# Axial attention in a ten-layer kernel: six SBUF-to-SBUF transfers for the maxima's rows, scores eleven steps behind, and the last scores in two pairs of PSUM banks

## The reference, cut to what matters

```python
q = (x @ Wq).reshape(b, n, 32, 8)
k, v = jnp.split(ctx @ Wkv, 2, axis=-1)      # each to (b, n, 32, 8)
q = apply_axial_rope(q, pos_map)
k = apply_axial_rope(k, ctx_pos_map)
logits = jnp.einsum('bqhd,bkhd->bhqk', q, k) * scale
w = jax.nn.softmax(logits, axis=-1)
attn = jnp.einsum('bhqk,bkhd->bqhd', w, v)
return attn.reshape(b, n, 256) @ Wout + bout
```

## Time and profile before

| | |
|---|---|
| median of 3 runs | 1564.13 us (1559.62 to 1566.8) |
| the profiled execution | 1560.38 us |
| its span, first to last instruction | 1558.6 us |
| PE, DVE, ACT busy over the whole span | 86%, 68%, 49% |
| mean granted TensorE clock | 0.928 of full speed |
| step -1 to the layer's last add | about 366 us to 533.9 us of the span |

### The profile page before, as it was taken

The page is one execution under the profiler, slowest core; times in us unless marked ns, Lnnn a source line. Parts: engine busy times, 40 slices in busy tenths (PEclk is TensorE's granted clock), DMA queues, the critical chain, the costliest instruction groups (busy, mean ns, idle before and its releaser), DMA issues.

```text
span 1558.6 us, 21496 instructions
## 1 busy us (share of the span) xinstructions
PE 1342.1 (86%) x6925; PEld 938.8 (60%) x6925; DVE 1053.0 (68%) x2217; ACT 761.3 (49%) x1887; POOL 209.0 (13%) x221
## 2 busy tenths in 40 slices
PE   8678759986898656899999779994999999869998
PEld 4344345553444334567676579983888888754554
DVE  6888968888776587788877533225666666666564
ACT  5677822445786474655554212223666666512221
POOL 0122220000000000312111064111111111010000
PEclk8799979996899887999999889997999999969999
DMA  5122140000000200000002179854211211000110
GB/s 194 68 95 81 75 189 1 0 1 1 5 4 5 78 0 1 1 1 34 35 1 79 38 281 332 300 206 159 102 67 67 74 67 61 34 0 17 33 33 27
DMA packets 36418, 111.02 MB, mean 71 GB/s; under 512 B 4693, under 2 KB 15966, under 8 KB 30992
## 3 DMA queue, kind: packets, MB, share of 16 engines
q1 hardware_dynamic: 34464, 105.75, 19.3%
q0 software_dynamic: 1872, 4.22, 0.7%
HBM read 84.66 MB, written 26.21 MB: 71 GB/s over the span
## 4 chain that ended last, share of the span: by engine, by line
PE 69%; DVE 16%; ACT 6%; issue 6%; DMA 2%; DVEq 0%; SPq 0%; POOL 0%; ACTq 0%; POOLq 0%
PE psum L3044 6%; PE psum L2356 5%; PE psum L2695 4%; PE psum L1938 4%; PE psum L871 4%; PE psum L2643 3%; PE psum L2673 3%; PE psum L1980 3%; PE psum L2721 3%; DVE roomA L752 3%; PE psum L3054 3%; PE psum L2365 2%; PE psum L1329 2%; PE psum L1970 2%; PE psum L2651 2%
## 5 line engine op out<-in xcount | busy, mean ns | idle before, releaser
L2760 ACT ACTIVATE roomA<-psum,roomA 128x256 f32<-128x256 f32 x128 | 71.0, 560 | 92.6 <-DVE roomA L2825 92.3
L1496 DVE TENSOR_REDUCE roomB<-psum 128x2 f32<-128x512 f32 x128 | 83.7, 688 | 35.9 <-PE psum L1329 34.8
L2026 ACT ACTIVATE roomA<-psum,roomA 128x128 f32<-128x128 f32 (+1 forms) x128 | 53.4, 427 | 88.3 <-DVE roomA L2101 88.1
L3044 PE MATMUL psum<-roomA,roomB 128*128 128x512 f32 (+1 forms) x192 | 89.4, 609 | 0.3 <-ACT roomA L3151 0.3
L2495 DVE SCALAR_TENSOR_TENSOR roomA<-roomA,psum 128x512 f32<-128x512 f32 x23 | 15.9, 690 | 99.1 <-ACT roomA L2400 99.1
L505 PE MATMUL psum<-roomB,own 128*128 128x256 f32 x256 | 64.9, 403 | 15.6 <-ACT roomB L604 15.3
L1938 PE MATMUL psum<-own,roomB 128*128 128x512 f32 x160 | 75.0, 594 | 3.4 <-DVE roomA L2093 2.1
L1901 POOL TENSOR_TENSOR roomA<-roomA 128x512 f32<-128x512 f32 x40 | 50.7, 1268 | 176.8 <-DVE roomA L2094 169.7
L505 PEld LDWEIGHTS psum<-roomB,own 128*128 128x128 f32 x256 | 50.8, 202 | 38.1 <-ACT roomB L604 20.6
L2695 PE MATMUL psum<-roomA 128*128 128x256 f32 x256 | 68.3, 389 | 6.0 <-DVE roomA L2837 4.4
L752 DVE TENSOR_TENSOR_SCAN roomA<-roomA 128x1024 f32<-128x1024 f32 x32 | 73.1, 2284 | 0.0
(11 more groups left out here) (509 smaller groups left out, 3396.5 us busy)
## 6 DMA issues: line engine op xcount, KB each, us to landing
roomB<-m_w_dram SPq DMA_DIRECT2D x12, 1536.0 KB
roomA<-m_w_dram SPq DMA_DIRECT2D x11, 1536.0 KB
a_kv_ready<-roomB SPq DMA_DIRECT2D x32, 512.0 KB, 3.1
roomA<-a_kv_ready SPq DMA_DIRECT2D x8, 1024.0 KB, 4.8
roomA<-a_kv_ready SPq DMA_DIRECT2D x16, 512.0 KB, 4.2
roomB<-a_w_dram SPq DMA_DIRECT2D x4, 1280.0 KB, 6.2
roomB<-f_w_dram SPq DMA_DIRECT2D x8, 624.0 KB, 3.8
m_rows<-roomA SPq DMA_DIRECT2D x1, 2978.5 KB, 15.7
```

Source lines behind the costliest of these rows:

```text
L1496: dve.tensor_reduce(maxneg[:, hp // 8, :, m, hp % 8], g.bank(m).rearrange("p (q k) -> p q k", k=S), AX.X, ALU.max, negate=True).then_inc(s ...
L3044: ins = pe.matmul(g.bank(bank, rows=m), w[:, kt, at:at + m], xg[:, n % 2, kt, half * HALF:(half + 1) * HALF], start=(kt == 0), stop=(kt == ...
```

## The change

- The DRAM tensor and the transfer into it go. Instead of store, wait and two loads, SP issues six transfers straight from `partsT` to `trQ`: one for each head m and part c, each from 8 partitions of 512 bytes into one partition's row of 4096 bytes. All six count on the same semaphore as the loads did (96 instead of 32 a batch).
- LAG goes from 13 to 11, so there are 83 steps instead of 85; scores, exponentials, `weigh`, `back` and `keep` all move two steps earlier against the maxima. M entries come one step earlier, in even steps (8, 16, ..., 64), behind the T entry of that step where there is one.
- From pair 53 on (SINGLE = 64 - 11, the first whose step has no `for_maxima`), scores use banks 0 and 1 and banks 2 and 3 in turn. They are issued in twos in odd steps, and pair n waits for the exponentials of pair n - 2 instead of n - 1. Pair 53 waits for all maxima to be read.
- `project_out` moves to banks 6 and 7 and is cut into two halves of a batch, in steps 66 to 71 one half each; batch 3 is done in step 81. The last A entry (step 79) waits for the adds of batches 0 to 2. The adds come in steps 68, 70, 72 and 82, and EARLY becomes 74.

```diff
-    shifts = g.nc.dram_tensor("a1_shifts", (B, 2, 48, S), BF16).ap()
-    LAG = 13
+    LAG = 11
...
-    ring += [(16 * t + 8 * hf + 9, "M", t, hf) for t in range(B) for hf in range(2)]
+    ring += [(16 * t + 8 * hf + 8, "M", t, hf) for t in range(B) for hf in range(2)]
...
-    OUT_STEP = [max(16 * t + LAG + 20, 53 + 2 * t, 64) + 2 for t in range(B)]
+    SINGLE = B * HP - LAG
+    OUT_STEP = [67, 69, 71, 16 * (B - 1) + LAG + 22]
+    HALF_OUT = [(OUT_STEP[t] - 1 + (r or t == B - 1), t, r) for t in range(B) for r in range(2)]
...
+    def score_bank(n):
+        return 0 if n >= SINGLE and (n - SINGLE) % 2 == 0 else 2
...
-                sp.dma_start(shifts[t, hf], partsT[:, hf, :]).then_inc(s["a1_stored"], 16)
-                sp.wait_ge(s["a1_stored"], 32 * t + 16 * hf + 16)
                 for m in range(2):
                     row = PARTS * HD + SLOT * m
-                    sp.dma_start(trQ[t % 2][row:row + 3, 8 * hf:8 * hf + 8, :],
-                                 shifts[t, hf].rearrange("(c m h) q -> c m h q", c=3, m=2)[:, m]).then_inc(s[f"a1_rows{hf}"], 16)
+                    for c in range(3):
+                        at = 16 * c + 8 * m
+                        sp.dma_start(trQ[t % 2][row + c:row + c + 1, 8 * hf:8 * hf + 8, :], partsT[at:at + 8, hf, :])\
+                          .then_inc(s[f"a1_rows{hf}"], 16)
...
             else:
+                if t == B - 1:
+                    pe.wait_ge(s["layer_done"], base + B - 1)
                 pe.wait_ge(s["a1_attn"], 4 * t + 4)
...
-            if n:
+            if n == SINGLE:
+                pe.wait_ge(s["a1_max_read"], 2 * B * HP)
+            elif n > SINGLE:
+                pe.wait_ge(s["a1_exp"], n - 1)
+            elif n:
                 pe.wait_ge(s["a1_exp"], n)
...
-        def project_out(t):
-            pe.wait_ge(s["a1_max_read"], 2 * B * HP)
-            pe.wait_ge(s["a1_at"], t + 1)
+        def project_out(t, r):
+            if t == 0 and r == 0:
+                pe.wait_ge(s["a1_mt"], 2 * B)
+                pe.wait_ge(s["a1_tr"], 8 * B)
+            pe.wait_ge(s["a1_at"], max(t, 2) + 1)
...
-            if 0 <= step - LAG < B * HP:
-                scores(step - LAG)
+            e = step - LAG
+            if 0 <= e <= SINGLE:
+                scores(e)
+            elif SINGLE < e < B * HP and (e - SINGLE) % 2 == 1:
+                scores(e)
+                if e + 1 < B * HP:
+                    scores(e + 1)
```

More of the change, by code:

```diff
@@ L1335, in scores @@
             if hp % 8 == 0:
-                pe.wait_ge(s[f"a1_rows{hp // 8}"], 32 * (t + 1))
-            if n:
+                pe.wait_ge(s[f"a1_rows{hp // 8}"], 96 * (t + 1))
+            if n == SINGLE:
[3 more added lines that the diff above has]
+            elif n:
                 pe.wait_ge(s["a1_exp"], n)
@@ L1341, in scores @@
                     rows = slice(SLOT * m, SLOT * m + ROWS)
-                    ins = pe.matmul(g.bank(2 + m)[:, kt * S:(kt + 1) * S], trK[t % 2][rows, hp, kt * P:(kt + 1) * P],
+                    ins = pe.matmul(g.bank(score_bank(n) + m)[:, kt * S:(kt + 1) * S], trK[t % 2][rows, hp, kt * P:(kt + 1) * P],
                                     trQ[t % 2][rows, hp, :], start=True, stop=True)
@@ L1367, in back @@
             ins.then_inc(s["a1_back"], 1)
-        def project_out(t):
-            pe.wait_ge(s["a1_max_read"], 2 * B * HP)
-            pe.wait_ge(s["a1_at"], t + 1)
+        def project_out(t, r):
[3 more added lines that the diff above has]
+            pe.wait_ge(s["a1_at"], max(t, 2) + 1)
             if t >= 2:
                 pe.wait_ge(s["layer_done"], base + t - 1)
[L1374 to L1379, removed]
+            i = 2 * t + r
+            for kt in range(KD):
+                ins = pe.matmul(g.bank(6 + t % 2)[:, r * D:(r + 1) * D], g.XT[:, kt, i * P:(i + 1) * P], w_out[:, kt, :],
+                                start=(kt == 0), stop=(kt == KD - 1))
+            if r:
+                ins.then_inc(s["a1_out"], 1)
         n = 0
@@ L1400, in tensor @@
                 n += 1
-            for t in range(B):
-                if OUT_STEP[t] == step:
-                    project_out(t)
+            for at, t, r in HALF_OUT:
+                if at == step:
+                    project_out(t, r)
         assert n == len(ring)
@@ L1431, in copies @@
                 if t:
-                    act.wait_ge(s[f"a1_rows{k}"], 32 * t)
+                    act.wait_ge(s[f"a1_rows{k}"], 96 * t)
                 act.copy(partsT[:, k, :], g.bank(6 + n % 2, rows=48).bitcast(BF16)[:, 0:S]).then_inc(s["a1_mt"], 1)
@@ L1444, in scalar @@
                     act.wait_ge(s["a1_pv"], (e - 4) // 2 + 1)
-                act.activation(slot(e).rearrange("p m k q -> p (m k q)"), g.ps[:, 2 * HALF:4 * HALF], ACT.Exp,
+                act.activation(slot(e).rearrange("p m k q -> p (m k q)"), g.ps[:, score_bank(e) * HALF:(score_bank(e) + 2) * HALF], ACT.Exp,
                                scale=float(HD) ** -0.5).then_inc(s["a1_exp"], 1)
@@ L1533, in vector @@
                     dve.wait_ge(s["a1_out"], t + 1)
-                    dve.tensor_tensor(xs, xs, g.bank(t % 2), ALU.add).then_inc(s["layer_done"], 1)
+                    dve.tensor_tensor(xs, xs, g.bank(6 + t % 2), ALU.add).then_inc(s["layer_done"], 1)
             if n == EARLY:
```

## The result

The changed kernel takes 1595.62 us (median of 4 runs, 1590.4 to 1599.78) against 1562.58 for the kernel before: a ratio of 1.0223 [1.0194, 1.0253]. It is slower by 2.2%, where 1557.9 was forecast. The profiled execution took 1594.02 us, with a span of 1592.3, so 33.7 us more than the span before. The layer, from the first maxima to the last add, went from 164.55 to 194.7 us; that is 30.2 of the 33.7.

A forecast was written before the change was run, and what follows sets the result against it. Three regimes: PE alone at half clock, shared steps with PE mostly busy, an end of waits. Pair 53 at 499.5 plus 17.5 + 9.7 + 1.0 gave 527.7 against 533.9: 1564.13 - 6.2 = 1557.9 us, range 1549.5 to 1564.5.

The forecast's parts named there:

- The rows' way: Six transfers from `partsT` to `trQ`: rows down 2.95 us after SP's start, 2.55 at best, 4.25 at worst.
- the prediction's own walk: Step-by-step pricing of the layer from first scores to last add, which ends at 527.7 against 533.9: -6.2 us.
- rival (a): Rows late at each cycle's step 3 and the first scores: +4.2 us, 1568.3, by the upper bound; chance 0.13.
- Rival (b): Gain at the end eaten by DVE's early norm and PE's halves, partly at half clock: net -0.7, 1563.4; chance 0.17.
- rival (c): Clock stays at 2.4 GHz in last shared steps and end, rows at lower bound: -11 us, 1553; chance 0.15.
- Start of the scores: First scores of the layer start at 390.1 instead of 392.59: -2.5 us.
- Cycle of eight: Eight shared steps take 15.93 us instead of 16.26; with 0.13 lost in each of seven halves, -1.0 in all.
- Cycles above 16.3 us, a wait of over 1 us for the rows at every eighth scores: Signs in the shared steps that would show the forecast wrong; it expected cycles of 15.9 to 16.1 us.
- Two more shared steps: Steps with both maxima and scores: 53 instead of 51, 2.07 us each, +4.1.
- The end: Pair 53 starts 0.8 later, then 17.5 us to the last `weigh` instead of 22.1, and +1.0 behind it.
- The exponentials of pairs 60 to 63: Sign at the layer's end: ACT runs these four without a gap, 4.1 us in all.
- the wait for DVE ahead of the last `keep`: Sign at the layer's end: `keep` of the last quarter waits for DVE itself, not for PE; +1.0 us.

The follow-up runs named there:

- e10: The changed kernel with 24 matmuls that nobody reads, run by PE before it waits for the rows: 1582.6 us, 1.0134 of the kernel before.
- e6: e1 with the M entry ahead of the T entry of its step: 1565.17 us, 1.0034 of the kernel before.
- e13: e6 with every eighth scores moved behind the first head's maxima, ahead of `weigh`: 1560.89 us, 0.9988 of the kernel before.
- e1: The changed kernel with its six transfers put back to store, wait and two loads through DRAM: 1569.85 us, 1.0044 of the kernel before.
- e4: The kernel before with the new end alone, rows through DRAM, scores thirteen steps behind: 1560.8 us, 0.9986 of the kernel before.
- e5: The changed kernel with the M entry ahead of the T entry of its step: 1579.1 us, 1.0128 of the kernel before.

## Why the prediction was wrong, point by point

**The step that failed** is the one under "The rows' way": issues bounded at 0.47 and taken at 0.31, from transfers with an end in DRAM. It was said that no row shows a transfer from SBUF to SBUF, and yet both bounds came from rows of another kind. The pitch measured 0.68, the landing 1.8 after the last issue, the whole 5.2 us (forecast 2.95, worst bound 4.25). The new way is 1.85 us longer than the one it replaces. The rule of the Trainium skill that stood against the change ("Rules for kernel authors" in DMA: Bandwidth & Descriptors, many small transfers into one) pointed the right way, and the traces agree with it: 48 issues of 635 ns took the place of 8 stores of 0.31 us and 16 loads of 0.25. The count alone doesn't decide it: at 0.31 an issue the six would take 5 x 0.31 + 1.8 = 3.35 us (my estimate, from the landing measured here), as long as the old way's 3.37. Why SBUF at both ends is dear the page doesn't say, and no run here tells. The 2.0 us that the prediction quotes from the Trainium skill stands there under "Anatomy of one DMA" for transfers that GpSimd issues; those of SP were seen done 1.1 to 1.4 us behind the issue.

**The sum with the right term.** Put 5.2 in place of 2.95 and the prediction's own walk gives 2.25 more for the first scores, and 2.25 more in each of seven halves, 18 in all: -6.2 becomes +11.8, 1576. Its rival (a) had this form, its bounds too near. The waits it names (2.38 a half) are the measured ones but for 0.4.

**What the walk lacked** is the other 21 us (33.0 between the medians, less 11.8): a wait of PE was priced at its own length. In the changed kernel it is followed by 7 or 14 us at half clock in which PE is the bound. Rival (b) priced a low clock in the end alone, rival (c) mentioned the clock only as a gain, and rival (a) left it out. e10 put its price at 13 us, by a filled wait at the same landing times. Of the remaining 8, 3 to 4 lie outside the layer, in code that is the same (1028.8 us there after, 1024.7 before, and 1024.7 to 1032.5 over all the profiled executions); the rest are the waits that came out 0.4 us a half longer than the walk has them, and what was not told apart.

**Start of the scores**, forecast 2.5 us earlier: measured 23.10 after the first maxima where it was 23.25, so nothing, as the rows were late by 3.00. By way of DRAM and with M first the gain is there: 20.4 in e6, 20.5 in e13.

**Cycle of eight**, forecast 15.93 before waits: right. e6 measured 15.87 without a wait, with M ahead of T. With M behind T, as the walk had it, e1's cycle from 446.50 to 463.06 took 16.56 at full clock, 0.90 of it the wait at its end. "Cycles above 16.3 us, a wait of over 1 us at every eighth scores" were named as what would prove the forecast wrong, and both came.

**Two more shared steps**, +4.1: not seen alone. e13's shared stretch, 107.2 us, stands against 105.45 + 4.1 - 1.0 = 108.6.

**The end.** Pair 53 to the last `weigh`, forecast 17.5: in the changed kernel 19.7 (533.39 to 553.12), of which 3.01 is a wait for the last rows, so 16.7 without. In e13 it is 17.9 (493.51 to 511.39) with a wait of 1.15. The size is right; this wait, at pair 56, was counted among the seven halves of the cycle and not in the walk of the end. The exponentials of pairs 60 to 63 do have gaps (1.51 and 0.28 ahead of them in the rows below), and the wait for DVE ahead of the last `keep` was right:

```profile
548.11 1.02 ACT L1462 ACTIVATE roomA<-psum 128x1024 f32<-128x1024 f32 x1 [1.51 <-PE psum L1352]
...
551.13 1.94 ACT L1462 ACTIVATE own<-psum 128x1024 f32<-128x1024 f32 x2 [0.28 <-PE psum L1352]
...
553.12 1.05 PE L1367 MATMUL psum<-own,roomA 128*9 128x256 f32 x16 [0.83 <-ACT own L1462]
...
557.41 0.29 DVE L1532 TENSOR_TENSOR roomB<-psum,roomB 128x128 f32<-128x128 f32 x1
557.85 0.63 PE L1324 MATMUL psum<-own,roomB 128*128 128x128 f32 x4 [2.31 <-DVE roomB L1532]
```

From the last `weigh` to the end of the last add it is 10.4 us, where 9.7 + 1.0 was forecast. The walk takes the last `weigh` at 16.9 for the 1.0 and at 17.5 in the sum; with 17.5 in both it would be 0.4, so the size is right and its working isn't. Alone, at LAG 13, the end's gain can't be told from nothing (e4, -0.14% with -0.32 to +0.03); by the prediction's own terms (0.8 - 4.6 + 1.0) it would be -2.8 us, 0.18%, which lies within that interval. In e4's trace 34.0 us pass from the end of the last maxima to the last add (498.9 to 532.9), where before has 35.85, so 1.9 less. The expectation of e4 had more than that sum gives.

**The arrangement** was expected to earn 6 us once the rows came in time. In e6 and e1 it didn't: at LAG 11 the 3.37 us of the way through DRAM land on the very step that needs them, and a slow store costs some 6 us there (22.27 against 15.87). At LAG 13, before and in e4, PE never waits for the rows; that was the cover whose loss the prediction did not price.

## What to carry to other kernels

Rows of another kind are no bounds for an operation that the trace does not show: where many instructions of an unseen kind stand in one queue, set the upper end well above the dearest related row (here 0.68 us from issue to issue against 0.47), and ask what it does to the sum. Slack ahead of a periodic transfer isn't idle time to be collected: compare the worst landing seen with the step that needs it, and price a miss at the wait plus the stretch at half clock that may come behind it. Where the slack must go, put the dependent matmuls behind other matmuls of the same step, as far as the next engine doesn't notice.

## What the hardware did that was not expected

- An issue on SP costs 0.62 to 0.64 us with 8 partitions of SBUF at one end and SBUF at the other, 0.50 to 0.52 for 48 partitions into 48 and for one row into one row, and 0.31 and 0.23 with DRAM as the target or the source. After the issue all are seen done in 1.1 to 1.4 us.
- PE waits of 2.76 and 3.18 us were each followed by 14 us at a granted clock of 0.52, while PE was busy 95% of the time; another of 2.76 by some 7 us; one of 1.29 by two stretches of 9.2 us at 0.58 and 0.67; three of 1.51 to 1.53 (e5) and one of 0.28 (e13) by none. Filling the wait with unread matmuls kept the clock at 1.00 in three cycles of five. The Trainium skill (TensorE: Matmul & The Clock Gate, "Part 1: The HAM clock gate") has the engine throttled unless recent activity releases it. The falls behind waits agree with that in kind; that the clock stayed low through 14 us in which PE was 95% busy, and stayed high behind e5's waits, these rows don't explain.
- A store of 24 KB to DRAM that is mostly seen done in 1.39 us took 3.02 (416.84 to 419.86) and 2.65 us in e6. In seven of 56 stores it took 2.27 us or more, and these seven alone have a 16 KB packet of the queue q8, called instruction, that starts within 1.4 us behind their issue.
